# Plain float32 operands in the 512-wide layer of a depthwise convolution and spiral scan, with sum, tanh and dot product in place in its PSUM bank

## The reference, cut to what matters

```
local = g[:, ci, :]
neigh = (g[:, ni, :] * nm[None, :, None]).sum(axis=1) / nc
u = jnp.concatenate([local, neigh], axis=-1)
y_sc = jnp.tanh(u @ w1 + b1) @ w2 + b2
g = g.at[:, ci, :].set(local + y_sc[:, None] * w_y[None, :])
```

## Time and profile before

| | |
|---|---|
| median of 3 runs | 5248.01 us |
| the runs | 5244.97, 5248.01, 5255.16 us |
| span of the profiled execution, first to last instruction | 5242.1 us |
| own time of the profiled execution | not listed apart from the three runs; the median is 5.9 us above its span |
| TensorE matmuls busy | 4812.6 us, 26981 records |
| VectorE busy | 4437.0 us, 7868 |
| ScalarE busy | 2045.2 us, 3253 |
| GpSimd busy | 1133.7 us, 1806 |
| mean granted TensorE clock | 0.973 of 2.4 GHz |
| DMA, mean | 126 GB/s |

### The profile page before, as it was taken

The page is one execution under the profiler, slowest core; times in us unless marked ns, Lnnn a source line. Parts: engine busy times, 40 slices in busy tenths (PEclk is TensorE's granted clock), DMA queues, the critical chain, the costliest instruction groups (busy, mean ns, idle before and its releaser), DMA issues.

```text
span 5242.1 us, 101723 instructions
## 1 busy us (share of the span) xinstructions
PE 4812.6 (92%) x26981; PEld 4082.9 (78%) x26981; DVE 4437.0 (85%) x7868; ACT 2045.2 (39%) x3253; POOL 1133.7 (22%) x1806
## 2 busy tenths in 40 slices
PE   4888888988888887999999999999999999999998
PEld 3777777887777776888888877788877887888776
DVE  6999999999999994777777877778777887888888
ACT  3555555555555552333333333333333333333332
POOL 1000000000000000333333333333333333333332
PEclk8999999999999998999999999999999999999999
DMA  4454544544444443433334333333333333333332
GB/s 104 159 164 153 163 154 155 169 163 154 152 159 148 156 151 150 118 114 112 115 109 114 116 111 111 109 110 115 108 105 104 112 109 104 107 112 104 106 100 72
DMA packets 253378, 661.81 MB, mean 126 GB/s; under 512 B 82210, under 2 KB 83234, under 8 KB 238370
## 3 DMA queue, kind: packets, MB, share of 16 engines
q1 hardware_dynamic: 209778, 552.76, 34.6%
q0 software_dynamic: 43056, 102.88, 6.1%
HBM read 347.00 MB, written 323.09 MB: 128 GB/s over the span
## 4 chain that ended last, share of the span: by engine, by line
PE 53%; issue 28%; DVE 17%; DVEq 1%; DMA 1%; SPq 0%; ACT 0%; POOL 0%; ACTq 0%; POOLq 0%
PE psum L785 13%; PE psum L783 13%; PE psum L784 13%; DVE dw_rows L568 9%; PE psum L771 6%; PE psum L779 3%; DVE bias_tmp L617 2%; DVE u_lo L602 2%; PE psum L744 2%; PE psum L750 2%; DVE relu_rows L638 1%; DVE gn_out L625 1%; DVE gn_out L610 0%; DVE win_tmp L643 0%; PE psum L728 0%
## 5 line engine op out<-in xcount | busy, mean ns | idle before, releaser
L568 DVE SCALAR_TENSOR_TENSOR dw_rows<-relu_rows,taps,dw_rows 128x896 f32<-128x896 f32 x1744 | 1863.0, 1145 | 104.0 <-ACT dw_rows L416 46.6
L783 PE MATMUL psum<-w_hi,u_hi 128*128 128x512 f32 x3588 | 1583.8, 441 | 0.0
L785 PE MATMUL psum<-w_hi,u_lo 128*128 128x512 f32 x3588 | 1413.6, 394 | 0.0
L468 ACT ACTIVATE gn_out<-gn_out 128x512 f32<-128x512 f32 x897 | 567.1, 632 | 2147.6 <-DVE gn_out L610 1840.4
L784 PE MATMUL psum<-w_lo,u_hi 128*128 128x512 f32 x3588 | 1401.5, 391 | 0.0
L377 POOL DMA_INDIRECT out<-gn_out,idx_col x897 | 881.9, 983 | 2034.7 <-POOLq L383 1375.4
L610 DVE SCALAR_TENSOR_TENSOR gn_out<-v_row,s_col,psum 128x512 f32<-128x512 f32 x897 | 668.7, 746 | 456.3 <-PE psum L785 387.0
L744 PE MATMUL psum<-pw,dw_rows 128*128 128x256 f32 x3136 | 846.1, 394 | 0.0
L750 PE MATMUL psum<-ident,dw_rows 128*128 128x128 f32 x6216 | 836.5, 279 | 0.0
L750 PEld LDWEIGHTS psum<-ident,dw_rows 128*128 128x128 f32 x6216 | 757.7, 145 | 87.2 <-issue 8.2
L785 PEld LDWEIGHTS psum<-w_hi,u_lo 128*128 128x128 f32 x3588 | 676.5, 189 | 155.4
(11 more groups left out here) (75 smaller groups left out, 2728.3 us busy)
## 6 DMA issues: line engine op xcount, KB each, us to landing
gn_out<-scratch SPq DMA_DIRECT2D x3588, 64.0 KB
scratch<-gn_out SPq DMA_DIRECT2D x112, 1792.0 KB, 5.7
x_tok<-x SPq DMA_DIRECT2D x112, 896.0 KB, 6.6
out<-gn_out,idx_col POOLq DMA_INDIRECT x897
relu_rows<-coef SPq DMA_DIRECT2D x1, 5830.5 KB
gn_out<-L_conv_w SPq DMA_DIRECT2D x2, 512.0 KB, 7.6
store_idx<-store_row SPq DMA_DIRECT2D x1, 448.5 KB, 7.7
w_row<-L_conv_w SPq DMA_DIRECT2D x1, 256.0 KB, 6.0
```

Of the source, the lines that this page charges most:

```text
L468: act.activation(th[:, cc % 2, :], pre_s[:, cc % 2, :], ACT.Tanh).then_inc(th_ready, 1)
L568: ins = dve.scalar_tensor_tensor(out=dst, in0=src, scalar=w, in1=dst, op0=ALU.mult, op1=ALU.add)
L783: pe.matmul(bank, hi, w1_hi[:, k, :], start=False, stop=False)
L785: last = pe.matmul(bank, lo, w1_hi[:, k, :], start=False, stop=k == 2 * CK - 1)
```

## The change

The layer's operands are no longer split. `w1_sb` and `u_sb` are plain float32, TensorE does one float32 product for each block, and VectorE's low parts are gone, in the setup and in each tile. The addition of s, tanh and the dot product now read and write the tile's PSUM bank 4 + c % 4; `pre_s` and `th` are gone. So TensorE waits, for a bank, until the dot product of tile c-4 is done (`y_ready`) and no longer only its addition, and for its operand on ScalarE's copy (`u_copied`) and no longer on VectorE. The waits of the addition for the tanh two tiles back, and of tanh for the dot product two tiles back, which kept `pre_s` and `th` from being overwritten, are gone.

```diff
-        w1_hi = sb("w1_hi", [P, 2 * CK, HID], f32r)
-        w1_lo = sb("w1_lo", [P, 2 * CK, HID], f32r)
-        u_hi = sb("u_hi", [P, U_SLOTS, 2 * C], f32r)
-        u_lo = sb("u_lo", [P, U_SLOTS, 2 * C], f32r)
+        w1_sb = sb("w1_sb", [P, 2 * CK, HID])
+        u_sb = sb("u_sb", [P, U_SLOTS, 2 * C])
...
-            act.sem_inc(th_ready, 2)
+            act.sem_inc(u_copied, 4)
...
-            def high_part(c, cc):
+            def copy_u(c, cc):
                 act.wait_ge(u_ready, c + 1)
                 act.wait_ge(pre_ready, c + 1)
-                act.activation(u_hi[:, cc % U_SLOTS, :], psum[:, cc % 4, :], ACT.Copy).then_inc(hi_ready, 1)
+                act.activation(u_sb[:, cc % U_SLOTS, :], psum[:, cc % 4, :], ACT.Copy).then_inc(u_copied, 1)
 
             def tile(c, cc, *_):
                 if not isinstance(c, int) or c + AHEAD < TILES:
-                    high_part(c + AHEAD, cc + AHEAD)
-                act.wait_ge(pres_ready, 4 + c + 1)
-                act.wait_ge(y_ready, c + 1)
-                act.activation(th[:, cc % 2, :], pre_s[:, cc % 2, :], ACT.Tanh).then_inc(th_ready, 1)
+                    copy_u(c + AHEAD, cc + AHEAD)
+                act.wait_ge(pres_ready, c + 1)
+                act.activation(psum[:, 4 + cc % 4, :], psum[:, 4 + cc % 4, :], ACT.Tanh).then_inc(th_ready, 1)
...
                 w = w1a[:, k, :] if k < CK else psum[:, 2 + k, :]
-                link(dve.tensor_copy(w1_hi[:, k, :], w))
-                link(dve.tensor_tensor(w1_lo[:, k, :], w, w1_hi[:, k, :].bitcast(f32), ALU.subtract))
+                link(dve.tensor_copy(w1_sb[:, k, :], w))
...
-            dve.sem_inc(pres_ready, 4)
-            dve.sem_inc(y_ready, 2)
+            dve.sem_inc(y_ready, 4)
             dve.sem_inc(s_ready, 1)
-            dve.sem_inc(lo_ready, 4)
...
-            def low_part(c, cc):
-
-                dve.wait_ge(hi_ready, c + 1)
-                slot = cc % U_SLOTS
-                dve.tensor_tensor(u_lo[:, slot, :], psum[:, cc % 4, :], u_hi[:, slot, :].bitcast(f32),
-                                  ALU.subtract).then_inc(lo_ready, 1)
-
             def add_s(c, cc, level, g):
 
                 dve.wait_ge(pre_ready, 4 + c + 1)
-                dve.wait_ge(th_ready, c + 1)
                 dve.wait_ge(s_ready, level + 1)
-                dve.scalar_tensor_tensor(out=pre_s[:, cc % 2, :], in0=v_row[:, :], scalar=s_col[:, g:g + 1],
+                dve.scalar_tensor_tensor(out=psum[:, 4 + cc % 4, :], in0=v_row[:, :], scalar=s_col[:, g:g + 1],
                                          in1=psum[:, 4 + cc % 4, :], op0=ALU.mult,
                                          op1=ALU.add).then_inc(pres_ready, 1)
 
             def dot(c, cc, y):
 
-                dve.wait_ge(th_ready, 2 + c + 1)
-                dve.tensor_tensor_reduce(out=prod, in0=th[:, cc % 2, :], in1=w2_row[:, :], scale=1.0,
+                dve.wait_ge(th_ready, c + 1)
+                dve.tensor_tensor_reduce(out=prod, in0=psum[:, 4 + cc % 4, :], in1=w2_row[:, :], scale=1.0,
...
                 add_s(c, cc, level, g)
-                if not isinstance(c, int) or c + AHEAD < TILES:
-                    low_part(c + AHEAD, cc + AHEAD)
                 if j:
                     dot(c - 1, cc - 1, y_of(l, g + 1))
...
-                pe.wait_ge(lo_ready, c + 1)
+                pe.wait_ge(u_copied, c + 1)
...
             def hidden(c, cc):
 
-                pe.wait_ge(lo_ready, 4 + c + 1)
-                pe.wait_ge(pres_ready, c + 1)
+                pe.wait_ge(u_copied, 4 + c + 1)
+                pe.wait_ge(y_ready, c + 1)
                 bank = psum[:, 4 + cc % 4, :]
                 pe.matmul(bank, pick[:, :], bias_rows[:, C:C + HID], start=True, stop=False)
                 for k in range(2 * CK):
-                    hi = u_hi[:, cc % U_SLOTS, P * k:P * (k + 1)]
-                    lo = u_lo[:, cc % U_SLOTS, P * k:P * (k + 1)]
-                    pe.matmul(bank, hi, w1_hi[:, k, :], start=False, stop=False)
-                    pe.matmul(bank, hi, w1_lo[:, k, :], start=False, stop=False)
-                    last = pe.matmul(bank, lo, w1_hi[:, k, :], start=False, stop=k == 2 * CK - 1)
+                    last = pe.matmul(bank, u_sb[:, cc % U_SLOTS, P * k:P * (k + 1)], w1_sb[:, k, :],
+                                     start=False, stop=k == 2 * CK - 1)
                 last.then_inc(pre_ready, 1)
```

More of the change, by code:

```diff
@@ L126, in build @@
           load_row, store_row, coef, wrap, side, scratch, out):
-    f32, f32r = mybir.dt.float32, mybir.dt.float32r
+    f32 = mybir.dt.float32
     bf16, i32 = mybir.dt.bfloat16, mybir.dt.int32
@@ L184, in build @@
         x_tile = part("x_tile", TILE_SLOTS, 2 * C)
-        pre_s = part("pre_s", 2, HID)
-        th = part("th", 2, HID)
         o_tile = part("o_tile", OUT_SLOTS, C)
@@ L226, in build @@
         u_ready = sem("u_ready")
-        hi_ready = sem("hi_ready")
-        lo_ready = sem("lo_ready")
+        u_copied = sem("u_copied")
         pre_ready = sem("pre_ready")
@@ L456, in _ @@
             row_steps(act, step, ROWS - 1 + OUT_LAG)
-            def high_part(c, cc):
+            def copy_u(c, cc):
                 act.wait_ge(u_ready, c + 1)
                 act.wait_ge(pre_ready, c + 1)
-                act.activation(u_hi[:, cc % U_SLOTS, :], psum[:, cc % 4, :], ACT.Copy).then_inc(hi_ready, 1)
+                act.activation(u_sb[:, cc % U_SLOTS, :], psum[:, cc % 4, :], ACT.Copy).then_inc(u_copied, 1)
             def tile(c, cc, *_):
                 if not isinstance(c, int) or c + AHEAD < TILES:
-                    high_part(c + AHEAD, cc + AHEAD)
-                act.wait_ge(pres_ready, 4 + c + 1)
-                act.wait_ge(y_ready, c + 1)
-                act.activation(th[:, cc % 2, :], pre_s[:, cc % 2, :], ACT.Tanh).then_inc(th_ready, 1)
+                    copy_u(c + AHEAD, cc + AHEAD)
+                act.wait_ge(pres_ready, c + 1)
+                act.activation(psum[:, 4 + cc % 4, :], psum[:, 4 + cc % 4, :], ACT.Tanh).then_inc(th_ready, 1)
             for c in range(AHEAD):
-                high_part(c, c)
+                copy_u(c, c)
             tile(0, 0)
@@ L621, in finish @@
             def finish(c, cc, y):
-                dve.wait_ge(y_ready, 2 + c + 1)
+                dve.wait_ge(y_ready, 4 + c + 1)
                 dve.wait_ge(out_stored, c + 1)
@@ L661, in y_of @@
                 return y_lvl[:, level % 2, g:g + 1]
-            for c in range(AHEAD):
-                low_part(c, c)
             centre_y = y_of(1, 0)
             add_s(0, 0, 0, 0)
-            low_part(AHEAD, AHEAD)
             dot(0, 0, centre_y)
-            dve.wait_ge(y_ready, 2 + 1)
+            dve.wait_ge(y_ready, 4 + 1)
             dve.tensor_copy(hist[0:B, GROUPS - 1, 2 * PAD + 1:2 * PAD + 2],
@@ L802 @@
 SETUP_T = SETUP_CST + 4
-SETUP_V = SETUP_T + 4 * CK + 1 + 2 + (1 + 6) + (1 + 3) + 1
+SETUP_V = SETUP_T + 2 * CK + 1 + 2 + (1 + 6) + (1 + 3) + 1
 CONV_TAPS = [(1, 0), (1, 2)] + [(ky, kx) for ky in (0, 2) for kx in range(3)]
```

## The result

The changed kernel takes 5765.99 us (median of 4 runs, 5764.56 to 5767.74) against 5247.4 before: a ratio of 1.0984, 95% interval 1.0969 to 1.1000. The forecast was 5801, with a range of 5751 to 5853. The profiled execution has a span of 5762.7 us and a time of its own of 5764.56. The 520.6 us that the span grew by are made as follows: the scan, from the first to the last addition of s, 3659.9 us for 3144.9, +515.0; what lies ahead of it, 2094.2 for 2088.6, +5.6; what follows, no change.

A forecast was written before the change was run, and what follows sets the result against it. TensorE was taken to bound the layer: 801 x 4.09 + 36, 64 x 4.09 and 31 x 4.09 make 3701 us against 3145, +556, less 3 of setup; 5242.1 + 553 + 5.9 = 5801 us, range 5751 to 5853.

The forecast's parts named there:

- What bounds: Spiral layer: TensorE sets the pace at 3.40 us a tile, except at the end with two tiles or one a level.
- The price of a plain product: TensorE in the scan: a plain float32 product is two halves, 0.857 us; four take 3.43 us against 2.74, tile 4.09.
- The first rival: TensorE's products: a plain float32 product costs only half as much, so the kernel gets faster, 4372 us; chance 0.03.
- The low parts: VectorE in the scan: 897 subtractions of 683 ns leave; last stages become TensorE-bound and 34.2 us of bias matmul waits go.
- a fixed 36: First 801 tiles: 36 of the 70 us above 3.40 a tile, called TensorE's own stalls and slow matmuls, stay.
- the time around the span: Start and end around the profiled span plus the run's own scatter: 5.9 us, kept unchanged in the sum.
- In place: Addition, tanh and dot product on the PSUM bank: no change for each, bounded at 0.1 us either way.
- The held bank: Rival at loop turns: TensorE waits for the dot product of c-4, up to 3 us each, about 5915 us; chance 0.04.
- Two tiles and one tile a level: Last stages of the scan: without low parts both become TensorE-bound at 4.09 us a tile; single-tile chain about 3.8.
- Setup: Ahead of the scan: four subtractions of 0.69 us and their link go from a chain TensorE waits for, -3 us.

The follow-up runs named there:

- e3: The kernel before without VectorE's low parts, the third product of each block taking the high part again, still twelve float32r products: 5177.31 us, ratio 0.9863.
- e1: The changed kernel with sum, tanh and dot product through pre_s and th in SBUF as before, plain float32 products kept: 5766.64 us, ratio 1.0985.
- e5: The changed kernel with float32r operands, one single product for each block, low parts of both operands left out of the result: 4547.67 us.
- e8: The changed kernel with eight more matmuls a tile, of bfloat16 zeros, 64 columns wide: 6068.19 us.
- e2: The kernel before with sum, tanh and dot product in the bank, twelve float32r products and low parts kept: 5226.77 us, ratio 0.9957.
- e6: The changed kernel with products of tile c waiting for the dot product of c-2, as if they had two banks, not four: 6662.05 us.
- e7: The kernel before with transposes, high and low parts made three tiles ahead of the products instead of two (AHEAD 3): 5220.38 us, ratio 0.9943.

## Why the prediction was right, and where it wasn't

*What bounds.* Right: TensorE set the pace of the scan before and does after. e3 took the low part from VectorE and left the steady tile at 3.40 us; e1 shows the products alone to be the loss.

*The price of a plain product.* Right: 0.857 us from the setup's line 716, eight halves 3.43 us in the scan. The tile is 3659.9 / 896 = 4.085 and not 4.09, 5 us over the scan. The Trainium skill ("FP8 and Floating Point Precision", TensorE Precision Notes) gives true float32 four passes. The trace shows no passes, only two records of 0.43 us; four passes would be 0.214 each. Valued at the float32r spacing they would have given 200 us too much, as the forecast said. The first rival, half the price, is refuted. Its 4372 us wouldn't have been reached either: e5 shows a tile of 2.68 us, set by the loads, where the rival had 2.37 for TensorE.

*The low parts.* The direction was right, the size too small. The step that failed is "The remaining 36 are TensorE's own stalls and the matmuls after a stall that run at the lower clock", which the sum then carried over as a fixed 36. By e3 only 14.6 of them stay without low parts; the rest went with the low part's lateness, since the slow matmuls behind such a wait had the same cause. And the 14.6 didn't carry over either: the changed kernel has none. By e8 they most likely hang on the number of TensorE's records between two turns of the loop, which the change cuts from 34 to 26 a tile. I had counted what each instruction takes and not how many there are. The 35 us by which 5801 was too high are this 36, 4.5 of rounding the tile up and 2.6 in what was set for the time around the span, less 8.6 of a scan that starts later than summed, and half a us of rounding. The 8.6 hid part of the error, by luck; the range held the result because its lower end let the 36 go.

*In place.* Taken at nothing, and nothing in the changed kernel (e1). On the kernel before it is worth 20 us (e2), which no step had foreseen. The two waits that order two-slot buffers are the likely cause, where TensorE's cover is thin; that isn't shown, since the shorter tanh came with them.

*The held bank.* No wait for it with four banks, neither with a tile of 4.085 nor on the faster tile of e2; 1.17 us at a tile with two banks (e6). The rival's mechanism exists, its place is two tiles away.

*Two tiles and one tile a level.* Right: 4.085 and 4.04 us a tile, TensorE-bound; without low parts a single tile needs 3.81 for its chain (e3), against 3.8 worked out.

*Setup.* The setup is shorter by 2.8 us, as the start of the first transposes shows (55.80 us for 58.60 in the timelines), but the scan starts 5.6 us later and not 3 earlier. In the six kernels with unsplit operands the first addition comes at 2091.8 to 2098.4 us, in the five others at 2088.6 to 2091.3. From the first bias matmul to the transposes behind its products it is 4.25 us before and 5.43 after, which is 1.2 of it. e6 has the same code ahead of the scan as the changed kernel, and its first addition comes at 2098.4 for 2094.2: single traces differ by 4 us there without any change. So the rest may be scatter, or a cost of the change in the convolution; it stays open.

## What to carry to other kernels

On an engine that sets the pace, price a new form of instruction by an instance of it that the kernel already runs, even eight records in the setup, and look whether it is one record or two. Splitting float32 by hand into three float32r products of 0.228 us beats one plain product of 0.857 by 0.17 us, as long as the split itself hides beside TensorE. When a change has two halves, time them apart: here one lost 10% and hid that the other gains 0.4%. A name behind a wait is that of what ended last: check in the code whether the engine needed it (e2). And a stall "for issue" at a loop's turn isn't a constant of the loop; here it came and went with the number of TensorE's records in the body.

## What the runs showed of the hardware that I had not expected

TensorE ran 897 tiles, 27 turns of hardware loops among them, without one stall at nine instructions in the code a tile, once the first tile was loaded, and stood up to 3.9 us at turns with seventeen (e7). Between 1680 and 1904 records a turn lies the step from none to over 2 us. Eight more matmuls of 64 columns with their own weight loads cost 0.32 us together, 0.04 each, in a tile of plain float32 products (e8). SyncE issued a load every 0.67 us, which bounds a tile of four loads at 2.68 (e5). Tanh from bank to bank takes 582 ns where SBUF to SBUF took 632.
